# The order of the first layer: projection and split two batches ahead, earlier in a round, and the sums for the ternary weights in the prologue

## The reference

```
x = x + attention0(wkv(x, f, f, w, u, cond))     # softmax attention, 16 heads of 16, causal
x = x + ffn0(wkv(x, f, f, w2, u2, cond))         # ternary weights, result quantised by one scale
x = x + attention1(wkv(...))                     # triangular solve per head, then attention
x = x + ffn1(wkv(...))                           # 8 experts, the best two of each token
```

## Time and profile before

| | us |
|---|---|
| device time, median of 3 runs | 846.26 (845.45 to 848.48) |
| device time of the profiled execution | 847.45 |
| its span, first to last instruction | 845.6 |
| busy: TensorE matmul, VectorE, ScalarE, GpSimd | 506.5, 552.5, 299.8, 227.6 |
| mean granted TensorE clock, share of full speed | 0.763 |

### The profile page before, as it was taken

The page is one execution under the profiler, slowest core; times in us unless marked ns, Lnnn a source line. Parts: engine busy times, 40 slices in busy tenths (PEclk is TensorE's granted clock), DMA queues, the critical chain, the costliest instruction groups (busy, mean ns, idle before and its releaser), DMA issues. The chain is left out here.

```text
span 845.6 us, 17910 instructions
## 1 busy us (share of the span) xinstructions
PE 506.5 (60%) x7444; PEld 419.3 (50%) x7444; DVE 552.5 (65%) x1066; ACT 299.8 (35%) x716; POOL 227.6 (27%) x320
## 2 busy tenths in 40 slices
PE   0333256288695866426466465758877660899980
PEld 0332144266484645325354344546655450899970
DVE  6549789687699796776627763556564155667733
ACT  3222535244354630053650332442313150365520
POOL 2000000000000000103855826813850026044343
PEclk9865568699788967757677676857979655899995
DMA  8255001404000010760070014200001062656214
GB/s 312 91 112 112 1 1 32 81 1 102 12 2 1 1 50 1 158 143 4 2 151 7 8 43 79 46 6 9 10 9 12 5 276 80 250 193 234 84 52 124
DMA packets 52067, 61.30 MB, mean 72 GB/s; under 512 B 25409, under 2 KB 45393, under 8 KB 47505
## 3 DMA queue, kind: packets, MB, share of 16 engines
q1 hardware_dynamic: 50176, 55.15, 24.2%
q0 software_dynamic: 1808, 4.99, 2.0%
HBM read 45.24 MB, written 13.63 MB: 70 GB/s over the span
## 5 line engine op out<-in xcount | busy, mean ns | idle before, releaser
L873 PE MATMUL psum<-arena 32*32 32x16 f32 (+17 forms) x5608 | 351.3, 269 | 257.3 <-DVE arena L1544 67.1
L873 PEld LDWEIGHTS psum<-arena 128*32 128x32 f32 (+7 forms) x5608 | 279.3, 127 | 328.3 <-DVE arena L1544 70.7
L1979 POOL TENSOR_TENSOR arena<-arena 128x31 f32<-128x31 f32 (+15 forms) x124 | 69.1, 558 | 9.7
L1977 POOL TENSOR_TENSOR arena<-arena 128x31 f32<-128x31 f32 (+15 forms) x124 | 63.6, 513 | 9.7
L1615 DVE TENSOR_REDUCE arena<-psum 128x2 f32<-128x512 f32 (+1 forms) x48 | 41.4, 861 | 21.5 <-PE psum L873 21.1
L1335 ACT ACTIVATE psum<-psum,arena 128x256 f32<-128x256 f32 (+7 forms) x128 | 45.8, 371 | 22.2 <-DVE arena L1605 22.2
L1957 POOL DMA_DIRECT2D arena<-wq x1 | 0.9, 862 | 191.7 <-PE psum L873 191.7
L1304 ACT ACTIVATE arena<-psum 128x512 f32<-128x512 f32 (+1 forms) x48 | 35.3, 735 | 47.0 <-PE psum L873 46.9
L1514 DVE TENSOR_TENSOR_SCAN arena<-arena 128x255 f32<-128x255 f32 x64 | 42.5, 727 | 9.6 <-ACT arena L1247 9.4
L1990 POOL TENSOR_TENSOR fc_second_parts<-arena,fc_first_parts 128x2048 fp32r<-128x2048 f32 x6 | 27.9, 4654 | 63.7 <-ACT fc_first_parts L1425 63.7
L1412 ACT ACTIVATE psum<-psum,arena 128x256 f32<-128x256 f32 x64 | 24.8, 458 | 48.1 <-PE psum L873 48.1
(11 more groups left out here) (180 smaller groups left out, 955.7 us busy)
## 6 DMA issues: line engine op xcount, KB each, us to landing
arena<-fc SPq DMA_DIRECT2D x16, 1024.0 KB, 5.2
arena<-parts SPq DMA_DIRECT2D x40, 256.0 KB, 4.6
parts<-arena SPq DMA_DIRECT2D x16, 384.0 KB, 3.3
arena<-parts SPq DMA_DIRECT2D x40, 128.0 KB, 5.6
dispatched<-arena SPq DMA_DIRECT2D x1, 2048.0 KB, 19.0
arena<-arena SPq DMA_DIRECT2D x128, 8.0 KB, 1.8
arena<-dispatched SPq DMA_DIRECT2D x8, 256.0 KB, 3.1
expert_rows<-arena SPq DMA_DIRECT2D x8, 256.0 KB, 2.2
```

The source lines that it names most:

```text
L873: return nc.tensor.matmul(out, lhsT, rhs, start=start, stop=stop)
L1977: link(G_.tensor_tensor(tmp, A3[:, k + 1:BLK, k:k + 1].to_broadcast([P, rows, w]), X3[:, k:k + 1, 0:w].to_broadcast([P, rows, w]), ALU.mult))
L1979: ins = G_.tensor_tensor(X3[:, k + 1:BLK, 0:w], X3[:, k + 1:BLK, 0:w], tmp, ALU.add)
```

## The change

The two lists of `first_layer` are reordered.

- Prologue: values(1), wkv(0,1), scale and back(0,1) stand before proj(0,0) in every list; keys 2 and 3, values 2 and wkv(0,2) before proj(0,1). largest(0) follows VectorE's part of proj(0,0), largest(1) precedes that of proj(0,1). limit(0) and limit(1) both come right after the first scores of batch 0, ternary(0) after `max`, and ternary(1) in round 0, after VectorE's part of proj(0,2). The prologue draws 4 steps of the stream.
- Rounds: gate(0,b+2) opens the round; proj(0,b+2) stands after the second scores instead of after the fourth, VectorE's part of it one recurrence step later; split(0,b+2) stands before pv instead of after it. Rounds 0 to 2 draw 8 steps, round 3 draws 7, and after it 2 are drawn instead of 1. The rest of the stream (5 steps, from wkv(3,3) on) comes after ("fc2", 3) in ORDER.
- The scratch of ScalarE's two sums per matrix is a slice of the prob tile instead of `tern_tmp`. The wait for the first matrix's square moves from ScalarE's `limit` to VectorE's `ternary`.

```diff
--- before.py
+++ after.py
@@ -158,24 +158,25 @@
                 both(("scale", *step[1:]))
 
     both(("keys", 0), ("values", 0), ("wkv", 0, 0), ("scale", 0, 0), ("keys", 1), ("back", 0, 0), ("weigh", 0, 0), ("gate", 0, 0))
+    both(("values", 1), ("wkv", 0, 1), ("scale", 0, 1), ("back", 0, 1))
     others(("proj", 0, 0))
-    both(("values", 1), ("wkv", 0, 1), ("scale", 0, 1), ("back", 0, 1))
     vec(("proj", 0, 0))
-    both(("split", 0, 0), ("weigh", 0, 1), ("gate", 0, 1))
+    both(("largest", 0), ("split", 0, 0), ("weigh", 0, 1), ("gate", 0, 1), ("keys", 2), ("keys", 3), ("values", 2))
+    recur(1)
     others(("proj", 0, 1))
-    both(("keys", 2), ("keys", 3), ("values", 2))
+    both(("values", 3), ("largest", 1))
+    vec(("proj", 0, 1))
+    both(("scores", 0, 0, 0), ("limit", 0), ("limit", 1))
     recur(1)
-    vec(("proj", 0, 1))
-    both(("values", 3), ("largest", 0), ("split", 0, 1), ("scores", 0, 0, 0), ("largest", 1), ("scores", 0, 0, 1))
-    recur(2)
-    both(("scores", 0, 0, 2), ("limit", 0), ("scores", 0, 0, 3), ("minus", 0, 0), ("max", 0, 0))
+    both(("scores", 0, 0, 1), ("split", 0, 1), ("scores", 0, 0, 2))
     recur(1)
-    both(("ternary", 0), ("limit", 1))
+    both(("scores", 0, 0, 3), ("minus", 0, 0), ("max", 0, 0), ("ternary", 0))
     recur(1)
-    both(("ternary", 1))
 
     for b in range(B):
         nxt, third, last = b + 1 < B, b + 2 < B, b - 1
+        if third:
+            both(("gate", 0, b + 2))
         both(("probs", 0, b, 0))
         if nxt:
             both(("scores", 0, b + 1, 0))
@@ -185,37 +186,37 @@
         both(("probs", 0, b, 1))
         if nxt:
             both(("scores", 0, b + 1, 1))
+        if third:
+            others(("proj", 0, b + 2))
         if b:
             others(("wo", 0, last))
         recur()
+        if third:
+            vec(("proj", 0, b + 2))
         if b:
             vec(("wo", 0, last))
             both(("gate", 1, last))
+        else:
+            both(("ternary", 1))
         both(("probs", 0, b, 2))
         if nxt:
             both(("scores", 0, b + 1, 2))
-        if third:
-            both(("gate", 0, b + 2))
         recur()
         both(("probs", 0, b, 3))
         if nxt:
             both(("scores", 0, b + 1, 3), ("minus", 0, b + 1))
-        if third:
-            others(("proj", 0, b + 2))
-        recur()
         if b:
             others(("fc1", last, 0), ("fc1", last, 1))
         if nxt:
             others(("max", 0, b + 1))
+        if third:
+            both(("split", 0, b + 2))
+        recur()
+        recur()
+        both(("pv", 0, b))
         if b == 0:
             both(("alpha", 0), ("alpha", 1))
         recur()
-        if third:
-            vec(("proj", 0, b + 2))
-        both(("pv", 0, b))
-        recur()
-        if third:
-            both(("split", 0, b + 2))
         if b:
             others(("fc2", last))
         others(("otr", 0, b))
@@ -223,10 +224,11 @@
         if b:
             vec(("fc2", last))
         vec(("otr", 0, b))
-        recur()
+        if b < B - 1:
+            recur()
     last = B - 1
     both(("oT", 0, last))
-    recur()
+    recur(2)
     both(("wo", 0, last), ("gate", 1, last))
     others(("fc1", last, 0), ("fc1", last, 1), ("fc2", last))
     for step in stream:
@@ -333,7 +335,9 @@
 
 DVE_ORDER = lag(first_layer()[1] + ORDER[len(first_layer()[0]):])
 assert all([s for s in DVE_ORDER if s[0] == k] == [s for s in ORDER if s[0] == k]
-           for k in ("wkv", "weigh", "gate", "minus", "otr", "wo", "proj", "split", "scores"))
+           for k in ("wkv", "weigh", "gate", "minus", "split"))
+assert [s for s in DVE_ORDER if ring_of(s) and ring_of(s)[0] == "big" and "dve" in ring_of(s)[1]] == \
+    [s for s in ORDER if ring_of(s) and ring_of(s)[0] == "big" and "dve" in ring_of(s)[1]]
 
 
 def count_rings():
@@ -460,7 +464,8 @@
         vaug = [f[:, 0:QT * H * VW].rearrange("p (t h e) -> p t h e", t=QT, h=H) for f in vflat]
         uaug = uflat[:, 0:QT * H * VW].rearrange("p (t h e) -> p t h e", t=QT, h=H)
         vz = [f[:, 0:NS * Q4 * HD].rearrange("p (s q e) -> p s q e", s=NS, q=Q4) for f in vflat]
-        prob = take(H * (T + P)).rearrange("p (h t) -> p h t", h=H)
+        prob_flat = take(H * (T + P))
+        prob = prob_flat.rearrange("p (h t) -> p h t", h=H)
         otok = v3(take(QT * D), QT)
         oT = v3(take(CT * T), CT)
 
@@ -542,6 +547,9 @@
 
         def tern_tmp(i):
             return v3(tern_flat, (CT, MT)[i])
+
+        def tern_junk(i):
+            return v3(prob_flat[:, i * CT * HID:(i + 1) * CT * HID], (CT, MT)[i])
 
         def tern_part(i, k):
             return small[:, 8 + 3 * i + k:9 + 3 * i + k]
@@ -1358,10 +1366,8 @@
                     i = step[1]
                     w_ = (w1, w2)[i]
                     act.wait_ge(tern_lim, i + 1)
-                    if i:
-                        act.wait_ge(tern_abs, i)
                     for k, sign in enumerate((1.0, -1.0)):
-                        A(tern_tmp(i), w_, ACT.Relu, bias=limit(i, 1), scale=sign, accum_out=tern_part(i, k)).then_inc(tern_above, 1)
+                        A(tern_junk(i), w_, ACT.Relu, bias=limit(i, 1), scale=sign, accum_out=tern_part(i, k)).then_inc(tern_above, 1)
                         act.wait_ge(tern_above, 2 * i + k + 1)
                 elif kind == "ternary":
                     i = step[1]
@@ -1677,6 +1683,8 @@
                     tmp = tern_tmp(i)
                     settle()
                     dve.wait_ge(tern_above, 2 * (i + 1))
+                    if i:
+                        dve.wait_ge(tern_abs, i)
                     link(V.tensor_scalar(tmp, w_, limit(i, 1), None, ALU.is_lt))
                     V.scalar_tensor_tensor(out=w_, in0=w_, scalar=limit(i, 0), in1=tmp, op0=ALU.is_gt, op1=ALU.subtract
                                            ).then_inc(tern_cnt, 1)

```

## The result

The changed kernel takes 833.82 us at the median (831.76 to 835.15, 4 runs) against 846.77 (845.45 to 848.48, 4 runs): a ratio of 0.9844, 95% interval 0.9815 to 0.9873, so 13.2 us less. Forecast were 831 and a range of 824 to 841. The profiled execution took 831.76 us with a span of 830.0; 832.0 had been worked out for it. A second set of six runs, also beside the kernel before, gave 833.15 us and a ratio of 0.9814 (0.9774 to 0.9855).

A forecast was written before the change was run, and what follows sets the result against it. The prediction took VectorE's idle time before the first layer's last reduction as what could be won: -14.1 us there and -1.3 for a saved table load, from 847.45 to 832.0, or 831 at the median, range 824 to 841.

The forecast's parts named there:

- Prologue: Before round 0: VectorE's stalls of 9.44 and 11.03 us behind projections shrink by 7.4 and 10.1 us.
- the walk: First layer: each queue followed in its own order with measured step durations, putting the last gate at 279.7.
- Weight sums: Before the second weight matrix's ternary: own scratch lets ScalarE's passes run without waiting for the square, -3.9 us.
- Rounds: The four rounds: two DMA waits won, mostly given back to projection, oT and fc2; idle 29.6 us, -2.2.
- The end: After the last gate: scale(3,3) waits behind fc2 on ScalarE, so the last reduction starts at 310.9, -14.1 us.
- After it: Second layer's start: ScalarE already holds the exp table, so one table load is saved, -1.3 us.
- The table rule: ScalarE table switches: the skill's 2.66 us each against the trace's 1.28 us load without drain; sum differs 0 or 1.4.
- The first: Rival at the first layer's end: the end does not bind and everything removed passes through, 821.5 us; chance 0.08.
- The second: Rival in the rounds: the projection becomes the wait of each round, 841 us; chance 0.22.
- The third: Rival on TensorE: it falls to its lower clock, making the kernel slower, 861 us; chance 0.05.

The follow-up runs named there:

- e2: The kernel before with only the changed kernel's new prologue, rounds and end left as before: 827.13 us, ratio 0.9803.
- e8: e1 with the weight sums back on their old scratch: 824.58 us, ratio 0.9725.
- e7: e1 with split(0,b+2) back after pv and the recurrence step that follows: 836.23 us, ratio 0.9841.
- e1: The changed kernel with wkv(3,3) and its scale drawn right after the last gate, ahead of fc1 and fc2 of batch 3: 820.83 us, ratio 0.9717.
- e4: The kernel before with only its end changed, wkv(3,3) and its scale behind fc1 and fc2: 854.57 us, ratio 1.0094.
- e5: e1 with wkv(0,3) drawn after round 0's second score step instead of before its second probs: 816.19 us, ratio 0.9596.
- e9: The changed kernel with e1's and e5's edits plus weigh(2,2) ahead of fc2 in round 2 on VectorE: 809.99 us, ratio 0.9542.

## Why the prediction was right

- *Prologue.* Forecast: 24.4 us of waits become 2.9, round 0 at 79.4. In the first profile the gate starts at 77.67, with 1.2 us of these waits left: 0.55 at the projection's eviction, as above, and 0.6 at two later places (the 0.57 before the backward scan was in the walk, 26.4 to 27.0, but not in the 2.9). In the second profile of the changed kernel the gate starts at 79.85, and 2.00, 0.83 and 0.46 us are left of the waits that the forecast puts at 2.0, 0.4 and 0.5. The two profiles differ in the first projection, 6.89 and 8.35 us; the 8.30 of rows 6 was taken as a fixed cost and is not one (last section). e2 confirms the part: 21.3 us less at the end of the layer. That most of the whole gain is here was in the sum.
- *Weight sums.* The wait of 3.9 is gone. But the reason given, two passes that no longer wait for a square thanks to their own scratch, is only half of it: e8 keeps the old scratch and the old wait and is as fast. The order does it.
- *Rounds.* Forecast idle 29.6 us, measured 28.9, in the second profile 29.6. The terms: projection in round 0 6.9 against 6.68; wo in round 1 1.6 against 1.04, the gate behind it 3.1 against 3.34; second scores of round 2 4 against 3.98; fc2 in round 2 5.4 against 7.86. The last is the one that was mis-sized, and that the sum fits all the same is luck: the 0.9 for the projection of round 1 and the 1.2 for its scores did not come. VectorE came to fc2 3.9 us earlier than in the walk (221.9, not 225.8), fc2's eviction only 1.5 (229.7, not 231.2): TensorE starts fc1 at 208.99, behind ScalarE's probs and the scale at 205.76, and is busy almost without a gap until 228.66, whatever VectorE does meanwhile:

```profile
208.99 9.58 PE L881 MATMUL psum<-arena 128*128 128x256 f32 x32 [4.13 <-ACT arena L1313]
218.51 0.24 PE L1008 MATMUL psum<-arena 128*64 128x128 bf16 x1
218.68 9.98 PE L881 MATMUL psum<-arena 128*32 128x256 f32 x96
```

  The two DMA waits went as forecast, and e7 shows that the early split did it. Its price there was 11.7 us, about 11 in the forecast.
- *The end.* Forecast: a wait of about 10 from 291.6, the reduction at 310.9. Measured 10.76 from 289.8, and 309.41; in the second profile 10.81 and 312.31. e1 and e4 show the cause: 10.7 less between gate and reduction in one, 8.0 slower by the ratio in the other. This was the step at which the order of one queue (ScalarE's) decided, though nothing around it in the diff names a scale.
- *After it.* -1.3 for the table load, measured -1.5 (67.0 to 65.5). It does not show in the span: from the first block inverse to the end it took 454.3 instead of 452.8, within the scatter of that stretch (last section). So the 831.76 us of the profiled execution lies so near the 832.0 by luck: its first layer was 15.6 us shorter, not 14.1, and the rest of the second 1.5 longer.
- *The table rule.* Load and exp stand within 0.02 us of what is before them, at 297.84 too. The drain of about 1.38 us that the Trainium skill adds (ScalarE: Activation LUTs, What ACT_TABLE_LOAD costs) does not appear here either: from the end of the eviction to the start of the exp it is 1.32 us.
- *Rivals.* The first (the end does not bind, 821.5) would have been the outcome with e1's one line. The second (projection in each round) did not come: two waits of 7.2 us in all, 0.55 in the prologue and 6.68 in round 0; in the second profile of the changed kernel there were four of 10.6, with 2.00 and 0.83 in the prologue, 7.26 in round 0 and only 0.53 in round 1. The third needed the last fc2 at the lower clock; its 7.14 us at a granted clock of 1.00 are the same as before.

## What to carry over

Where each engine works through one written list, moving a step earlier or later moves every small instruction that stands behind it on each queue. Count the stream's steps before and after; one too few put a scale of 0.5 us behind a feed-forward stage and cost 8 to 11. A sum over the idle time of the busiest engine, walked through with the other queues' order, was right to 1.5 us here, some of it by luck; the terms that fail are those where another engine sets its own pace.

An early transfer can be worth its place even if what makes it early costs a wait: compare the pair, not the parts. And check that each part of a change earns something on its own: here the prologue alone did about as well as the whole, because the end lost at least what the rounds won, and the new scratch did nothing.

## What the hardware showed

- A granted clock of 1.00 in an early stretch of a profile can be the lack of a reading. The first projection (24 recorded matmuls, nothing on TensorE before it) took 6.89 us in the first profile of the changed kernel and 7.37 to 8.47 in the eleven others, and its row says 1.00. But the trace's records of the clock start only inside it, at 26.20 in the changed kernel and at 29.07 in the kernel before, both with a change to full clock, and at that moment the distance from one matmul to the next falls from 0.43 to 0.22 us. Four matmuls in 1 us is the pace that the projection of round 0 has at a granted clock of 0.50 (1.2 GHz), six to seven the one at 1.00 (2.4 GHz). Here are the stretch of the changed kernel, 1 us ahead of the change and 1 us behind it, and then the projection of round 0, whole and 1 us of it (length, busy, granted clock, DMA share, GB/s):

```profile
23.20:30.20 7.00, 6.89 (x24) 1.00 0.45 161
24.20:25.20 1.00, 1.00 (x4) 1.00 1.08 384
28.20:29.20 1.00, 1.00 (x6) 1.00 0.05 16
86.50:94.20 7.70, 7.70 (x27) 0.70 0.00 0
88.50:89.50 1.00, 1.00 (x4) 0.50 0.00 0
```

  So the 8.30 of rows 6 against the 5.42 of rows 8 is the time until the full clock came, and it differs from one execution to the next: seven matmuls start before the change in the first profile of the changed kernel, fourteen in the kernel before. What moves that moment no run here shows. With the second projection, which shows the same (8.18 and 8.91 us in the two profiles of the changed kernel), it accounts for the 2.2 us by which their round 0 is apart, out of 2.9 at the end of the layer.
- The projection of round 0 began at a granted clock of 0.50 in the six profiles in which TensorE had been idle for 4.23 or 4.24 us just before it; its stretch of 40 matmuls took 8.8 to 9.4 us. In e5 and e9 it followed the probs after 0.27 and 0.52 us, at 1.00, and took 6.56. In the changed kernel the clock fell at 84.23, within the idle time, and came back at 91.06. The shorter gap and the faster clock go together; that the gap alone does it, and not the changed order of the work ahead of it, is not shown.
- The second layer, the same instructions in all kernels, took 446.7 to 455.9 us from the first block inverse to the end. The granted clock over it was 0.78 in the shortest (e9) and 0.74 in one of the longest (the changed kernel again, 455.7), but 0.77 in the longest (e5, 455.9), so the clock is not all of it. A single profile's span can't show an effect under 5 us here; the end of the first layer scatters less, but still by 3 (310.13 and 313.03 for the changed kernel).
